# Row maxima of a run's first batch in pairs of heads, node biases in three places, and the second batch's projections after four heads

## The reference

```python
x = x + L0_attn(layernorm(x))                 # random-feature attention
x = x + L0_xattn(layernorm(x), ctx, mask)     # q from x, k and v from ctx, masked query rows, softmax
x = x + L0_ffn(layernorm(x))                  # three hard-routed trees q, k, v, one attention, a fourth tree f
x = x + L1_attn(layernorm(x))                 # causal softmax attention
x = x + L1_xattn(layernorm(x), ctx)           # softmax attention against ctx
x = x + L1_ffn(layernorm(x))                  # product-key experts: top 16 of 32 x 32 per head, 8 heads

# the attentions of runs 1 and 2
corr = einsum('bhqd,bhkd->bhqk', q, k) * scale    # 8 features a head
prob = softmax(corr, axis=-1)                     # causal in L1_attn
out  = einsum('bhqk,bhkd->bhqd', prob, v) @ Wo

# a tree: 8 levels, node logits with a bias
logit = einsum('bsd,bsd->bs', x, nw[node]) + nb[node]
node  = 2 * node + 1 + (logit > 0)
```

## Time and profile before

| | |
|---|---|
| median of 3 runs | 764.22 us (763.98 to 765.98) |
| profiled execution, its own time | 762.6 us |
| its span, first to last instruction | 760.9 us, mean TensorE clock 0.933 |
| busy: TensorE matmul, weight load | 638.0 us (84%), 490.3 us (64%) |
| busy: VectorE, ScalarE, GpSimd | 601.0 us (79%), 441.3 us (58%), 323.3 us (42%) |
| first run: first score row, last of batch 4's reductions | 99.05 us, 110.72 us |
| feed-forward stage: first leaf's gather, last leaf's matmuls | 185.17 us, 409.25 us |
| second run: first score row, first columns | 411.35 us, 427.32 us |

### The profile page before, as it was taken

How to read it: one execution, slowest core, us unless ns; L and a number is a source line. 1 busy time by engine, 2 the same in 40 slices (tenths; PEclk the granted TensorE clock), 3 DMA queues, 4 the chain that set the end, 5 groups by cost and what they waited for, 6 DMA issues and landing times. The chain is left out here.

```text
span 760.9 us, 14555 instructions
## 1 busy us (share of the span) xinstructions
PE 638.0 (84%) x4837; PEld 490.3 (64%) x4837; DVE 601.0 (79%) x2439; ACT 441.3 (58%) x1064; POOL 323.3 (42%) x318
## 2 busy tenths in 40 slices
PE   4869858878898899988878899899879788888898
PEld 2547515444587668777676566655547677778897
DVE  5894777685899899996689777887448789999984
ACT  1333106556498778889874455566645755555562
POOL 4150432922434232331165122221014788888892
PEclk9985659899799999999999999999999899999999
DMA  8000021101999799996552211111000000000000
GB/s 256 5 1 3 24 62 50 44 1 55 417 359 376 281 377 367 358 419 227 205 231 70 63 48 45 47 46 46 2 1 0 2 1 5 5 5 5 4 6 8
DMA packets 38931, 86.07 MB, mean 113 GB/s; under 512 B 3993, under 2 KB 30146, under 8 KB 30664
## 3 DMA queue, kind: packets, MB, share of 16 engines
q0 software_dynamic: 9216, 69.47, 23.4%
q1 hardware_dynamic: 29640, 15.67, 7.6%
HBM read 74.43 MB, written 0.52 MB: 99 GB/s over the span
## 5 line engine op out<-in xcount | busy, mean ns | idle before, releaser
L852 ACT ACTIVATE arena<-arena,hact 128x128 f32<-128x128 f32 x512 | 155.4, 388 | 1.0
L732 ACT ACTIVATE arena<-psum 128x512 f32<-128x512 f32 (+1 forms) x192 | 101.3, 561 | 51.1 <-PE psum L1495 50.5
L627 POOL TENSOR_TENSOR arena<-arena 128x1024 f32<-128x1024 f32 x64 | 121.2, 1912 | 20.1 <-DVE arena L1339 14.6
L1192 DVE CUSTOM_DVE_ANT_0 arena<-arena,fx 128x128 f32<-128x128 f32 x384 | 106.5, 344 | 5.7 <-DMA arena<-tab_q,leaf_no 3.6
L899 ACT ACTIVATE psum<-arena,tneg 128x1024 f32<-128x1024 f32 x64 | 71.4, 1117 | 58.0 <-DVE arena L1339 27.5
L1897 PE MATMUL psum<-arena 128*128 128x128 f32 x688 | 87.0, 284 | 17.8 <-DVE arena L1339 16.9
L988 DVE TENSOR_REDUCE rowmax<-psum 128x2 f32<-128x512 f32 x128 | 81.3, 686 | 22.1 <-PE psum L1477 20.5
L1897 PEld LDWEIGHTS psum<-arena 128*128 128x128 f32 x688 | 83.0, 199 | 22.1 <-DVE arena L1339 14.5
L1477 PE MATMUL psum<-arena 128*128 128x256 bf16 (+1 forms) x384 | 73.6, 283 | 16.6 <-DVE rowmax L988 11.2
L1784 PE MATMUL psum<-identf,arena 128*128 128x128 f32 x544 | 75.5, 292 | 7.6 <-ACT arena L852 6.8
L1784 PE MATMUL psum<-arena,identf 128*128 128x128 f32 x544 | 72.1, 283 | 6.5 <-ACT arena L852 6.0
(11 more groups left out here) (237 smaller groups left out, 1173.2 us busy)
## 6 DMA issues: line engine op xcount, KB each, us to landing
arena<-parts SPq DMA_DIRECT2D x144, 64.0 KB
w_sb<-attn_w SPq DMA_DIRECT2D x1, 768.0 KB, 8.2
x<-x_in SPq DMA_DIRECT2D x1, 512.0 KB, 4.1
fx<-ctx_in SPq DMA_DIRECT2D x1, 512.0 KB, 5.1
picked<-mask_in SPq DMA_DIRECT2D x1, 512.0 KB, 6.2
wq_sb<-peer_wq SPq DMA_DIRECT2D x1, 512.0 KB, 8.1
down_sb<-table_down SPq DMA_DIRECT2D x1, 512.0 KB, 9.1
up_sb<-table_up SPq DMA_DIRECT2D x1, 512.0 KB, 8.7
```

The costliest lines, as they stand in the source:

```text
L627: nc.gpsimd.tensor_tensor(grid[k % 3].rearrange("p (i j) -> p i j", i=PK), sim[:, t, h, :].unsqueeze(2).to_broadcast([P, PK, PK]), sim[:, ...
L732: nc.scalar.activation(probs[k % (2 * HG)][:, 0:w], bank(2 + k % 2, 0, w), ACT.Exp, scale=float(D) ** -0.5).then_inc(probs_ready, 1)
L852: a = nc.scalar.activation(w, w, ACT.Copy, scale=hact[i % 2][:, l:l + 1])
L1192: i = nc.vector.tensor_tensor_reduce(w, w, src, 1.0, r[:, LW * E + l:LW * E + l + 1], ALU.mult, ALU.add, hid[g % 4][:, l:l + 1])
```

## The change

- `score_rows` of a run's first batch uses four banks, `h % 4`, and waits only from head 4 on, for the pair of heads two before. In the second run its first head waits for the tree logits in those banks to have been read.
- `row_max_pair` takes the maxima of two heads in one reduction over two banks: 1024 elements, or 2 x 384 where causal. A causal head is now reduced as three groups of 128, into `rowmax` with three rows instead of two, in the paired form and in `row_max` of the later batches, and `max_parts` of a causal batch begins with the maximum of two of the rows.
- The node biases are done in three places on GpSimd: the first cast and subtraction after `split(6)`; the first multiplication and the second cast after the run's work; the rest behind a wait for the maxima parts of batch 6 (`mparts_ready` 3).
- The projections of batch 9 move on TensorE from the end of the feed-forward stage to behind the first four heads' rows of batch 8.
- GpSimd's `clear(0)` and `clear(1)` ahead of the second run wait also for `xn_ready` 11, the normalised batch 10.

```diff
@@ -98,7 +98,7 @@
         resid_f = sb("resid_f", [P, 2, S])
         parts = [sb(f"parts{i}", [P, 3, 2, S], bf16) for i in range(2)]
         vaug = [sb(f"vaug{i}", [P, SUB, H, VW]) for i in range(4)]
-        rowmax = [sb(f"rowmax{i}", [P, SUB, H]) for i in range(2)]
+        rowmax = [sb(f"rowmax{i}", [P, 3, H]) for i in range(2)]
         negmax = sb("negmax", [P, SUB, H])
         remax = sb("remax", [P, SUB, H])
         mparts = [sb(f"mparts{i}", [P, SUB, 3, H], bf16) for i in range(2)]
@@ -341,7 +341,7 @@
         TENSOR_AT = {("score", 0): 7, ("turn", 2): 8, ("mix", 0): 10, ("turn_f", 0): 11,
                      ("turn", 3): 12, ("score", 1): 14, ("mix", 1): 16, ("turn_f", 1): 18, ("score", 2): 20,
                      ("mix", 2): 22, ("turn_f", 2): 23, ("score", 3): 25, ("mix", 3): 26, ("turn_f", 3): 27,
-                     ("next", NEXT[0]): 28, ("next", NEXT[1]): 32}
+                     ("next", NEXT[0]): 28}
         SCALAR_AT = {("out", 2 * B - 1): 1, ("turn", 2): 8, ("weigh", 0): 10, ("mix", 0): 10, ("turn_f", 0): 11,
                      ("turn", 3): 12, ("weigh", 1): 16, ("mix", 1): 16, ("turn_f", 1): 18, ("weigh", 2): 22,
                      ("mix", 2): 22, ("turn_f", 2): 23, ("weigh", 3): 26, ("mix", 3): 26, ("turn_f", 3): 27,
@@ -541,6 +541,9 @@
                 for n in range(first, last + 1):
                     if n + 2 <= last:
                         split(n + 2)
+                        if first == B and n == first:
+                            node_cast(0)
+                            node_rest(0)
                     if n + 3 <= last:
                         power(n + 3)
 
@@ -582,6 +585,7 @@
                 power(NEXT[1])
                 power(NEXT[1] + 1)
                 pool.wait_ge(leaf_done, len(ORDER) - 1)
+                pool.wait_ge(xn_ready, NEXT[1] + 2)
                 clear(NEXT[1] % 3)
                 clear((NEXT[1] + 1) % 3)
                 split(NEXT[1])
@@ -636,6 +640,25 @@
                         if h == 7 and t + 2 < T:
                             pair_sums(t + 2)
 
+            node_parts = bias_p[:, 9 * P:NB]
+
+            def node_cast(j):
+
+                if j == 0:
+                    pool.wait_ge(in_tab, 32)
+                link(nc.gpsimd.tensor_copy(nbias_w, nbias_sb))
+
+            def node_rest(j):
+
+                link(nc.gpsimd.tensor_tensor(nbias_sb, nbias_sb, nbias_w, ALU.subtract))
+
+            def node_row(j):
+
+                row = identf[0:3, j:j + 1].to_broadcast([3, 4 * NODES])
+                link(nc.gpsimd.tensor_tensor(nbias_w if j else node_parts, nbias_w, row, ALU.mult))
+                if j:
+                    link(nc.gpsimd.tensor_tensor(node_parts, node_parts, nbias_w, ALU.add))
+
             pool.wait_ge(kmax_all, 1)
             power(B)
             power(B + 1)
@@ -645,17 +668,14 @@
             power(B + 2)
             split(B + 1)
             run(*RUNS[0])
-            pool.wait_ge(in_tab, 32)
-            p = bias_p[:, 9 * P:NB]
-            for j in range(3):
-                row = identf[0:3, j:j + 1].to_broadcast([3, 4 * NODES])
-                link(nc.gpsimd.tensor_copy(nbias_w, nbias_sb))
-                if j < 2:
-                    link(nc.gpsimd.tensor_tensor(nbias_sb, nbias_sb, nbias_w, ALU.subtract))
-                link(nc.gpsimd.tensor_tensor(nbias_w if j else p, nbias_w, row, ALU.mult))
-                if j:
-                    link(nc.gpsimd.tensor_tensor(p, p, nbias_w, ALU.add))
-            nc.gpsimd.tensor_copy(nbias_w[:, 0:1], p[:, 0:1]).then_inc(nbias_ready, 1)
+            node_row(0)
+            node_cast(1)
+            pool.wait_ge(mparts_ready, 3)
+            node_rest(1)
+            node_row(1)
+            node_cast(2)
+            node_row(2)
+            nc.gpsimd.tensor_copy(nbias_w[:, 0:1], node_parts[:, 0:1]).then_inc(nbias_ready, 1)
             ffn()
             run(*RUNS[1])
             peer()
@@ -982,12 +1002,22 @@
                 k = (n - B) * H + h
                 dve.wait_ge(rows_ps, k + 1)
                 if stage(n) == 2:
-                    nc.vector.tensor_reduce(rowmax[n % 2][:, 0, h:h + 1], bank(k % 2, 0, P), AX.X, ALU.max)
-                    i = nc.vector.tensor_reduce(rowmax[n % 2][:, 1, h:h + 1], bank(k % 2, P, P + S), AX.X, ALU.max)
+                    i = nc.vector.tensor_reduce(rowmax[n % 2][:, :, h], bank(k % 2, 0, 3 * P).rearrange("p (s n) -> p s n", n=P),
+                                                AX.X, ALU.max)
                 else:
-                    i = nc.vector.tensor_reduce(rowmax[n % 2][:, :, h], bank(k % 2).rearrange("p (s n) -> p s n", s=SUB),
+                    i = nc.vector.tensor_reduce(rowmax[n % 2][:, 0:SUB, h], bank(k % 2).rearrange("p (s n) -> p s n", s=SUB),
                                                 AX.X, ALU.max)
                 i.then_inc(rows_max, 1)
+
+            def row_max_pair(n, h):
+
+                dve.wait_ge(rows_ps, (n - B) * H + h + 2)
+                two = psum[:, h % 4 * BANK:(h % 4 + 2) * BANK].rearrange("p (a c) -> p a c", a=2)
+                if stage(n) == 2:
+                    o, r = rowmax[n % 2][:, :, h:h + 2], two[:, :, 0:3 * P].rearrange("p a (s n) -> p a s n", n=P)
+                else:
+                    o, r = rowmax[n % 2][:, 0:SUB, h:h + 2], two.rearrange("p a (s n) -> p a s n", s=SUB)
+                nc.vector.tensor_reduce(o.rearrange("p s a -> p a s"), r, AX.X, ALU.max).then_inc(rows_max, 2)
 
             def max_parts(n):
 
@@ -995,7 +1025,9 @@
                 if n - 2 >= B:
                     dve.wait_ge(mt_ps, n - 1 - B)
                 mp = mparts[n % 2]
-                link(nc.vector.tensor_scalar(negmax[:, :, :], rowmax[n % 2][:, :, :], -1.0, None, ALU.mult))
+                if stage(n) == 2:
+                    link(nc.vector.tensor_tensor(rowmax[n % 2][:, 1, :], rowmax[n % 2][:, 1, :], rowmax[n % 2][:, 2, :], ALU.max))
+                link(nc.vector.tensor_scalar(negmax[:, :, :], rowmax[n % 2][:, 0:SUB, :], -1.0, None, ALU.mult))
                 link(nc.vector.tensor_copy(mp[:, :, 0, :], negmax[:, :, :]))
                 link(nc.vector.tensor_tensor(remax[:, :, :], negmax[:, :, :], mp[:, :, 0, :], ALU.subtract))
                 link(nc.vector.tensor_copy(mp[:, :, 1, :], remax[:, :, :]))
@@ -1082,8 +1114,8 @@
             resid(B - 1)
 
             def run(first, last):
-                for h in range(H):
-                    row_max(first, h)
+                for h in range(0, H, 2):
+                    row_max_pair(first, h)
                 max_parts(first)
                 for h in range(EARLY):
                     row_max(first + 1, h)
@@ -1460,16 +1492,24 @@
             def score_rows(n, h):
 
                 k = (n - B) * H + h
+                alone = n == run_of(n)[0]
                 if h == 0:
                     pe.wait_ge(stk_ready[n % 3], 16 * 13 * placed(n))
-                if k >= 2:
+                if alone and h == 0 and n > B:
+                    pe.wait_ge(dec_ready, B + 1)
+                    pe.wait_ge(decf_ready, B)
+                if alone:
+                    if h >= 4 and h % 2 == 0:
+                        pe.wait_ge(rows_max, k - 2)
+                elif k >= 2:
                     pe.wait_ge(rows_max, k - 1)
                 if h == 0 and n - run_of(n)[0] < 3:
                     pe.wait_ge(pad_ready[n % 3], 16 * (1 if n < 2 * B else 2))
                 q, kk = stk[n % 3][:, h, 0, :], stk[n % 3][:, h, 1, :]
-                o, causal = bank(k % 2), stage(n) == 2
+                at = h % 4 if alone else k % 2
+                o, causal = bank(at), stage(n) == 2
                 if causal:
-                    nc.tensor.matmul(diagonal_of(k % 2), identb[:, :], causal_q[:, :].unsqueeze(1).to_broadcast([P, 2, P]),
+                    nc.tensor.matmul(diagonal_of(at), identb[:, :], causal_q[:, :].unsqueeze(1).to_broadcast([P, 2, P]),
                                      start=True, stop=False, skip_group_check=True)
                 for s in range(SUB):
                     keys = P if causal and s == 0 else S
@@ -1666,6 +1706,8 @@
             def run(first, last):
                 for h in range(H):
                     score_rows(first, h)
+                    if first > B and h == 3:
+                        pre(first + 1)
                 max_turn(first)
                 pre_x(first + 2)
                 for h in range(EARLY):
```

## The result

Over 20 runs each, the changed kernel has a median of 761.33 us (758.5 to 762.59) and the kernel before 765.71 us (760.58 to 771.01). The ratio is 0.9939 [0.9922, 0.9956]: faster by 0.6%, some 4.7 us of 765.71. The profiled execution took 758.5 us (span 756.7, clock 0.928), against 762.6 (760.9, 0.933). That execution was the fastest of the changed kernel's 20. The time lies in the stated range of 754.2 to 762.0 us, near its upper end, but 0.5 us above the 756.3 to 760.8 that the prediction gave its main forecast. It is 3.0 us above the forecast's 758.3; 1.5 of that is the kernel before, whose median over 20 runs is that much above the 764.22 of three.

The account below looks back on a forecast made before the run. No engine bounds the whole span: TensorE's order sets the steady pace, while run starts alternate TensorE scores and VectorE maxima. Terms -5.1 - 1.1 + 0.5 - 0.2 = -5.9 us, from median 764.22 to 758.3 us; range 754.2 to 762.0.

Parts of the forecast that it names:

- main forecast: Whole kernel: 758.3 us, own range 756.3 to 760.8, chance 0.58.
- Sum: Whole kernel: the four parts, -5.1 - 1.1 + 0.5 - 0.2, give -5.9 us.
- only the stretch comes back: Rival: batch 6's casts recover their stretch, but TensorE's clock need not recover; 761.7 us, chance 0.14.
- Part 1: Node biases, batch 6: casts lose 3.47 us of stretch, full clock regains 1.6; -5.1 us, bounds 3.4 and 5.5.
- Part 2: Maxima of batch 4, two heads at a time: eight pairs in 9.4 us; -1.1 us, bounds -0.3 and -2.5.
- (1.225 + 1.1) / 2 = 1.17 us a pair: Batch 4's pairs: VectorE's 1.225 us and TensorE's about 1.1 take turns on one pair of banks.
- Part 3: Second run's start: maxima 2.1 us earlier, but batch 9's stack is late next; +0.5 us, bounds -2.1 and +2.
- four take 1.8: Second run's start: four heads of batch 8 at 0.44 us each delay batch 9's projections by 1.8 us.
- The 0.2 for the clock: Second run's start: TensorE stands about 0.7 us longer before batch 9's scores, costing another +0.2 us for the clock.
- Part 4: 48 later causal heads: one 384-element reduction replaces two, max_parts gains an operation; -0.2 us, bounds -1.5 and +0.5.
- The second run's start is won as well: Rival: maxima there done 2.1 us earlier count, and low clock of 99 to 112 us may end sooner; 755.0, chance 0.20.
- The slower case: Rival: TensorE stands 2.5 us before batch 9's scores, then stays at 1.2 GHz for a whole batch; 769, chance 0.04.

Follow-up runs that it names:

- e1: Kernel before with only the node biases in three places; 760.31 us against 763.13, ratio 0.9963.
- e10: Changed kernel with 45 unused matmuls in TensorE's batch 6 pause; 758.78 us, ratio 0.9926 to the kernel before.
- e2: Kernel before with its whole node bias chain behind the wait for batch 6's maxima parts, nothing moved forward; 765.40 us against 765.51, ratio 1.0015.
- e9: Changed kernel with 80 unused matmuls ahead of the first run's rows; 757.61 us, ratio 0.9921 to the kernel before.
- e3: Kernel before with only paired maxima in four banks and causal maxima by one operation; 763.02 us against 763.13, ratio 1.0001.
- e4: Changed kernel with batch 9's projections back at the feed-forward stage's end, without the memsets' wait for xn_ready; 757.97 us, ratio 0.9935 to the kernel before.
- e5: Changed kernel without the memsets' wait for xn_ready; 758.37 us, ratio 0.9941 to the kernel before.
- e7: Changed kernel with batch 9's projections back at the feed-forward stage's end and its split between the two memsets; 757.67 us, ratio 0.9916 to the kernel before.
- e8: Changed kernel with 40 unused matmuls behind the turn of batch 8; 760.18 us, ratio 0.9938 to the kernel before.
- e12: e14 with the six DMAs of k of batch 9's stack issued by ScalarE; 756.93 us, ratio 0.9899 to the kernel before.
- e14: Changed kernel with GpSimd's second memset moved behind the maxima parts of batch 8; 758.93 us, ratio 0.9924 to the kernel before.
- e13: e12 with unused matmuls in four TensorE pauses: 80 ahead of the first run, 45 in each of three others; 752.63 us, ratio 0.9843 to the kernel before.

## Why the prediction was right, and by how much its terms were off

**Sum.** Forecast -5.9 us, measured 4.7 by the ratio (3.4 to 6.0) and 4.2 between the profiles. Over the segments that the change touches the profiles give -5.6; the start and the end, which it does not touch, gave 1.7 back, and the feed-forward stage was 0.3 shorter. Of the -5.6, the 0.3 of mt 4 to 5 is the clock's scatter, and the two profiles' own differences at start and end are as large as some of the parts; so the sum is right to about a microsecond and no better. The measured time is also within a microsecond of the rival "only the stretch comes back" (761.7).

**Part 1 (-5.1): mechanism and size right, 1.4 of it given back.** The stretch went: 0.18 us twice. The turn moved by 3.0, not 3.47, because TensorE had columns to do until 144.85. The clock gave the remaining 2.0, where 1.6 stood, and e1 has 5.05 in all. The step left out is the next pause, 2.86 us before 159.92. I took full clock as won for good once it was back; in the changed kernel it was lost again there. e10 shows the price, 1.36 us. The norm's power found the chain done by 0.57 us, where I had 0.5, and e2 shows what lies beyond that margin.

**Part 2 (-1.1): the size right, its sum partly by luck.** -0.92. The pairs took 9.63 us for 9.4, 1.20 each with TensorE at half clock; e9 has 1.13 at full clock. But the sum's (1.225 + 1.1) / 2 = 1.17 us a pair can't be: VectorE alone, at the 1.225 put in, would need that much for each, 9.8 us for eight. The 1.225 was too much for a row of them: in e9 the next pair starts after 1.13. The two errors nearly cancelled.

**Part 3 (+0.5): sign wrong, -0.6.** The step that failed is "four take 1.8". They took 1.1 us (404.60 to 405.70), 0.27 a head. The 0.44 us is the busy time of a head that stands alone: in the stretch that it came from, TensorE waited on VectorE between heads. With four free banks a head's matmuls run into the next one's, and the busy time of one is no longer what each costs. With q and k 0.7 us sooner (out at 408.43), they and the memsets (408.65) ended together, and the split began at 408.60. SP began 4.76 us behind the last leaf, where I had 5.34. The rest held: batch 9's stack is late next, 9.54 us from first issue to first scores, where I had 9.7, and the maxima, 3.1 us earlier by now, wait for it. The 0.2 for the clock did not come: from the first scores of batch 9 to its maxima DMA it took 15.8 us before and after, since in before too the clock fell there, near 423.7. The same code in e9 and e10 has -0.4 and -0.1 for -0.6, so the gain is small; the forecast loss came in none of the three. Nor did I price the two parts apart: e3 and e4 show that the pairs alone give -1.4 and that the new order takes about 1 of it.

**Part 4 (-0.2): right, too small to matter.** mt 9 to mt 14 is 0.1 us shorter. The added maximum of two rows took 0.18 us where it is shown, and 0.7 us in all four batches. By the Trainium skill (SBUF — State Buffer, "Who interferes with whom") a GpSimd operation beside it could have shut it out; none stood there, and no row contradicts the rule. The casts, stretched beside GpSimd before and at 0.18 us without it, agree with it.

**Rivals.** "The second run's start is won as well" needed 2 us there and more from the clock at 99 us: 0.6, and the clock stayed at 0.50. "Only the stretch comes back" held in part, for the reason it did not name: the clock recovered and fell again. The slower case asked for half clock through a whole batch; it was at 0.50 from 416.1 to about 423 us, and it had fallen behind the pause ahead of the turn, before the 2.17 us wait for the stack began.

**Open.** Whether a pause of TensorE drops the clock: at the batch 6 pause of 2.85 us it fell in after and in e3, e4, e5, e7, e8, e9 and e12, and did not in before, e1 and e14; each of these is one profile. It moves a segment by 1.3 us where the low clock lasted 3.4 us (after) and by 2.3 where it lasted 6.8 (e4, e7), and decides what single parts of this change seem to be worth. What sets it was not found. Nor was why the clock, once low at a run's start, comes back 3.2 us behind mt 4 in one execution and 5.8 in another.

## What to carry to other kernels

Cut both traces at a landmark that every batch passes once and compare segments: that separated parts of 1 us that the run times could not. First find out from profiles of the same code how far a segment scatters: here 0.03 us in one and 0.5 to 0.9 in two others. The busy time of an operation that stands between waits is not its price when several follow each other: a head of 0.44 us cost 0.27, a reduction of 1.225 us cost 1.13. And when one wait is taken away, follow TensorE's clock through the next pause as well: there part of the gain can be given back. Where unused matmuls filled the pause itself (e9, e10, e13), the work right behind it ran at full clock; placed behind the pause (e8) they won nothing.

## What the runs showed of the hardware

Where the clock fell at the batch 6 pause of 2.85 us, the low level (1.2 GHz) lasted 3.4 us (after, e3, e5, e8, e9, e12) or 6.8 us (e4, e7), and began between 0.6 us before (e3) and 1.3 us after (e7) TensorE was back at work. At 542.4 us, in after, it fell with no pause of over 1.23 us in the 6 us ahead of it. In the 5.75 us pause ahead of the first run's rows, in after, it fell near 98.7 and stayed low for some 17 us, though TensorE was busy 8.33 of the 13 us from 99 to 112. 80 unused matmuls, 4.6 us of work where TensorE stood idle anyway, turned this into full clock. Twelve DMAs of 64 KB need 9.5 to 10.0 us from the first issue until TensorE may read when one queue issues them in 7.73 us (after, e9, e10, e14), and 9.1 us when two issue them in 5.3 (e12).
